# Edge scores of a graph layer: head sums of every fourth edge tile on ScalarE

## What is computed

```python
q = (x_norm @ Wq + bq).reshape(N, H, HD)      # N 1250, H 8, HD 64
k = (x_norm @ Wk + bk).reshape(N, H, HD)
scores = jnp.einsum('ehd,ehd->eh', q[origin], k[destination]) * SCALE
ws = scores * edge_weights
...
e = jnp.exp(ws - seg_max[origin])
```

## Time and profile before

| | |
|---|---|
| median of 3 runs | 2417.09 us |
| profiled execution, its own time | 2421.3 us |
| its span, first to last instruction | 2419.2 us |
| mean granted TensorE clock over the span | 0.846 of 2.4 GHz |
| stretch of `edge_scores` in it | about 527 to 802 us |
| busy over the span: PE / DVE / ACT / POOL | 79% / 52% / 20% / 33% |

### The profile page before, as it was taken

One profiled execution on the slowest core, in us unless ns is written; L12 is line 12 of the kernel. 1 busy time (PEld: TensorE's weight loads), 2 busy tenths in 40 slices (PEclk: granted clock), 3 DMA queues, 4 the chain that ended last, 5 costly groups with the idle time before them and its releaser, 6 DMA issues. The chain is left out here.

```text
span 2419.2 us, 23805 instructions
## 1 busy us (share of the span) xinstructions
PE 1921.7 (79%) x8175; PEld 1232.6 (51%) x8212; DVE 1265.2 (52%) x3309; ACT 476.3 (20%) x999; POOL 788.0 (33%) x697
## 2 busy tenths in 40 slices
PE   2499406976767579999896999989995999878876
PEld 2355203453333434444445888736554898655553
DVE  6565400438999679999102333433424274466423
ACT  3300000231111001111203222121212224343310
POOL 2077871026666067766202122101305301211100
PEclk8699757985676589999896899999997998887678
DMA  5022101026666156666101011011001000000001
GB/s 132 1 79 58 31 5 53 0 90 191 177 172 175 23 146 184 183 180 169 72 0 53 18 36 35 1 48 40 9 1 42 18 1 18 1 1 1 0 1 64
DMA packets 85241, 151.70 MB, mean 63 GB/s; under 512 B 34600, under 2 KB 39874, under 8 KB 85007
## 3 DMA queue, kind: packets, MB, share of 16 engines
q0 software_dynamic: 33280, 93.44, 14.5%
q1 hardware_dynamic: 51855, 56.91, 7.0%
HBM read 131.11 MB, written 19.02 MB: 62 GB/s over the span
## 5 line engine op out<-in xcount | busy, mean ns | idle before, releaser
L1074 POOL DMA_INDIRECT s_vbuf<-v_dram,s_recs x176 | 205.3, 1167 | 146.5 <-DVE s_vw L1102 75.3
L845 POOL DMA_INDIRECT s_kbuf<-k_dram,s_recs x176 | 167.5, 952 | 244.7 <-DMA s_recs<-rec_dram 149.3
L384 POOL DMA_INDIRECT rec_dram<-s_rec,s_rowid x160 | 199.7, 1248 | 143.0 <-issue 143.0
L1127 PE MATMUL s_pV<-s_vw,s_ohf 128*128 128x512 f32 x352 | 196.4, 640 | 0.0
L917 PE MATMUL s_psQ<-s_qh,s_ohT 128*128 128x512 f32 x176 | 111.8, 636 | 63.3 <-DVE s_prod L894 25.2
L894 DVE TENSOR_TENSOR s_prod<-s_psQ,s_kbuf 128x512 f32<-128x512 f32 x176 | 114.4, 683 | 24.5 <-remote 12.5
L1121 PE MATMUL s_pA<-s_ohd,s_ohb 128*128 128x512 bf16 (+1 forms) x491 | 117.0, 343 | 7.5 <-DVE s_ohf L1100 5.1
L1102 DVE TENSOR_TENSOR s_vw<-s_vbuf,s_W 128x512 f32<-128x512 f32 x176 | 120.5, 685 | 3.5 <-DMA s_vbuf<-v_dram,s_recs 3.5
L1121 PEld LDWEIGHTS s_pA<-s_ohd,s_ohb 128*128 128x128 bf16 x528 | 50.3, 98 | 127.0 <-issue 53.4
L618 PE MATMUL s_bank<-s_w,s_xnormT 128*128 128x512 f32 x240 | 114.9, 639 | 0.0
L684 PE MATMUL s_bank<-s_xnT,s_w 128*128 128x512 f32 (+1 forms) x96 | 37.2, 551 | 94.6 <-DMA s_w<-in_L_mix_WqkvT 94.6
(11 more groups left out here) (409 smaller groups left out, 4259.6 us busy)
## 6 DMA issues: line engine op xcount, KB each, us to landing
s_w<-in_L_ffn_W SPq DMA_DIRECT2D x16, 512.0 KB, 4.5
AT_dram<-s_A SPq DMA_DIRECT2D x10, 640.0 KB
s_w<-in_L_mix_WqkvT SPq DMA_DIRECT2D x3, 1024.0 KB
s_kbuf<-k_dram,s_recs POOLq DMA_INDIRECT x176
s_vbuf<-v_dram,s_recs POOLq DMA_INDIRECT x176
rec_dram<-s_rec,s_rowid POOLq DMA_INDIRECT x160
k_dram<-s_xn_rows SPq DMA_DIRECT2D x10, 256.0 KB
v_dram<-s_xn_rows SPq DMA_DIRECT2D x10, 256.0 KB
```

The lines of the kernel that those rows point to most:

```text
L384: nc.gpsimd.indirect_dma_start(out=b.rec_dram, out_offset=bass.IndirectOffsetOnAxis(ap=rowid[:, t:t + 1], axis=0), in_=rec[:, t, :], in_of ...
L845: nc.gpsimd.indirect_dma_start(out=kbuf[t % KB][:, :], out_offset=None, in_=b.k_dram, in_offset=bass.IndirectOffsetOnAxis(ap=recs[:, t, 2: ...
L1074: nc.gpsimd.indirect_dma_start(out=vbuf[t % VB][:, :], out_offset=None, in_=b.v_dram, in_offset=bass.IndirectOffsetOnAxis(ap=recs[:, t, 2: ...
L1127: nc.tensor.matmul(V[:, :], ohf[i][:, :], vw[i][:, :], start=False, stop=False, skip_group_check=True).then_inc(used[i], 1)
```

## The change

The tile with `t % 4 == 3`, the second of every odd pair, is multiplied into a buffer of its own (`act_prod`, two of them in turn), and VectorE does not reduce it. ScalarE sums it: eight copies of 64 columns onto themselves with an accumulated output that goes to `W[:, t, h:h+1]`. They come in two halves of four, behind the one-hot copies of the next two pairs: those of tile 4k+3 (pair 2k+1) behind the copies of pairs 2k+2 and 2k+3. The last tile's two halves stand behind the loop. The ring of `prod` shrinks from four buffers to three, and VectorE's waits are counted anew. TensorE's, GpSimd's and SyncE's instructions stay as they were.

```diff
-        sb, ps, s = b.tools(ctx, "loaded q_in qh ql identb oh0 oh1 tp0 tp1 ohT0 ohT1 qe0 qe1 prod0 prod1 red")
+        sb, ps, s = b.tools(ctx, "loaded q_in qh ql identb oh0 oh1 tp0 tp1 ohT0 ohT1 qe0 qe1 prod0 prod1 red act_red")
-        prod = [sb(f"prod{i}", [P, D]) for i in range(4)]
+        prod = [sb(f"prod{i}", [P, D]) for i in range(3)]
+        act_prod = [sb(f"act_prod{i}", [P, D]) for i in range(2)]
...
+            def head_sums(k, half):
+                t = 4 * k + 3
+                act.wait_ge(prod_s[1], t // 2 + 2)
+                for h in range(4 * half, 4 * half + 4):
+                    nc.scalar.activation(act_prod[k % 2][:, h * HD:(h + 1) * HD], act_prod[k % 2][:, h * HD:(h + 1) * HD], ACT.Copy,
+                                         accum_out=W[:, t, h:h + 1]).then_inc(s.act_red, 1)
...
                     nc.scalar.activation(ohT[i][:, :], psT[i][:, :], ACT.Copy).then_inc(ohT_s[i], 1)
+                if u >= 2:
+                    head_sums((u - 2) // 2, u % 2)
                 if u + 1 < NT:
                     high(u + 1)
+            for half in range(2):
+                head_sums(ST // 4 - 1, half)
+            act.wait_ge(s.act_red, H * (ST // 4))
...
-                    if t >= 4:
-                        dve.wait_ge(s.red, t - 3)
-                    nc.vector.tensor_tensor(prod[t % 4][:, :], psQ[i][:, :], kbuf[t % KB][:, :], ALU.mult).then_inc(prod_s[i], 1)
+                    if t % 4 == 3:
+                        out = act_prod[t // 4 % 2]
+                        if t >= 8:
+                            dve.wait_ge(s.act_red, H * (t // 4 - 1))
+                    else:
+                        out = prod[t % 4]
+                        if t >= 4:
+                            dve.wait_ge(s.red, 3 * (t // 4 - 1) + t % 4 + 1)
+                    nc.vector.tensor_tensor(out[:, :], psQ[i][:, :], kbuf[t % KB][:, :], ALU.mult).then_inc(prod_s[i], 1)
...
                     t = 2 * u + i
+                    if t % 4 == 3:
+                        continue
                     dve.wait_ge(prod_s[i], u + 2)
...
-            dve.wait_ge(s.red, ST)
+            dve.wait_ge(s.red, 3 * ST // 4)
```

## The result

The changed kernel takes 2422.94 us (median of 8 runs, 2421.49 to 2426.66), the kernel before beside it on the same chip 2415.82 us (8 runs, 2411.93 to 2419.83). The ratio is 1.0032 with a 95% interval of 1.0021 to 1.0043: slower by 0.3%, 7 us. The forecast was 2407 us with a range of 2396 to 2417, faster at 0.73. It is wrong in its number and in its sign. The profiled execution took 2422.19 us, its span 2420.4.

What follows compares the result with a forecast made beforehand. VectorE was taken to bound quiet pairs, with TensorE close behind at its lower clock. Terms -2.1 - 5.2 - 6.3 + 4.4 - 1.8 + 1.0 = -10.0 us gave 2407 us against the median of 2417.1, range 2396 to 2417.

Steps and rivals of the forecast that it cites:

- quiet pairs: From pair 10 on, pairs without late TensorE results: -5.2 us at the lower clock, -6.3 us at the higher.
- alternation: Products start 2.71 and 2.11 us apart in turn at the higher clock, 2.11 and 3.03 at the lower.
- granted clock: From pair 10 on, taken as 0.68: TensorE at its higher clock 36% of the time.
- first ten pairs: Start of the stage, with a low part of q: 3.31 us a pair becomes 3.01, together -2.1 us.
- tail: Last tile's eight sums on ScalarE end later than VectorE's last reduction did, delaying the next stage: +1.0 us.
- rival 3: ScalarE late: head sums of 0.55 us or more make it the bound, +13.4 us at 0.60, 2431 us; chance 0.07.
- stalls: Late TensorE results from pair 10 on: number kept at eleven, each about 0.4 us costlier, +4.4 us.
- rival 4: GpSimd's gathers take 1.35 us each, two 2.70: quiet pairs gain nothing, 2416 us; chance 0.06.
- rival 2: TensorE's clock stays high and VectorE alone bounds: -19.7 us, 2397 us; chance 0.20.

Runs made afterwards that it cites:

- e6: Changed kernel with only the first eight tiles gathered, all later products reusing their buffers: 2372.35 us, ratio 0.9796 to the kernel before.
- e2: Kernel before plus eight accumulating 64-column copies per two pairs on ScalarE, from a tile nobody else uses: 2421.91 us, ratio 1.0019.
- e3: Kernel before plus eight semaphore waits a pair on SyncE that nothing depends on: 2422.32 us, ratio 1.0021.
- e1: Changed kernel with ScalarE copying four columns per half instead of making four head sums: 2416.81 us, ratio 1.0002 to the kernel before.
- e5: Kernel before with only the first eight tiles gathered, all later products reusing their buffers: 2395.48 us, ratio 0.9884.
- e18: Changed kernel gathering only every second tile from the ninth tile on, fifth chip: 2373.30 us, ratio 0.9832 to the kernel before.
- e12: Changed kernel with gathers running four tiles ahead instead of eight, third chip: 2397.14 us, ratio 1.0001 to the kernel before.
- e16: Changed kernel with gathers running four tiles ahead instead of eight, fourth chip: 2420.39 us, ratio 1.0017 to the kernel before.
- e14: Changed kernel, nothing further edited, as a control on the fourth chip: 2424.58 us, ratio 1.0031 to the kernel before.

## Why the prediction was wrong

*What was right.* The quiet pairs: forecast 11.5 us of gain in 58 of them (5.2 and 6.3), measured 12.3 us in 62 by a slightly wider count. The alternation of 2.71 and 2.11 us at the higher clock came as written, at the lower one 2.97 and 2.11 to 2.18 for 3.03 and 2.11. The granted clock from pair 10 on was 0.70 (569 to 802 us), where 0.68 was taken. The first ten pairs took 36.6 instead of 37.8 us: 1.2 gained of 2.1. In the tail the last pair's product and the next stage's copy are 804.39 - 800.01 = 4.38 us apart instead of 3.62, 0.8 for the forecast's 1.0.

*ScalarE* (rival 3) was costed rightly. The view of the tile `act_prod` in the changed kernel:

```profile
L860 ACT ACTIVATE s_act_prod<-s_act_prod x352: 238/248/261, 537.0 to 803.0; 128x64 f32<-128x64 f32 x176
L860 ACT ACTIVATION_READ_ACCUMULATOR s_act_prod<-s_act_prod x352: 185/190/205, 537.2 to 803.2; 128x1 f32 x176
```

and the timeline of its end:

```profile
801.81 0.24 ACT L860 ACTIVATE s_act_prod<-s_act_prod 128x64 f32<-128x64 f32 x1
801.96 0.18 ACT L860 ACTIVATION_READ_ACCUMULATOR s_act_prod<-s_act_prod 128x1 f32 x1
802.05 0.24 ACT L860 ACTIVATE s_act_prod<-s_act_prod 128x64 f32<-128x64 f32 x1
...
803.15 0.18 ACT L860 ACTIVATION_READ_ACCUMULATOR s_act_prod<-s_act_prod 128x1 f32 x1
```

A sum follows the next after 0.24 us (taken 0.26), the accumulator's read is hidden, and the last ends at 803.33, 2.0 us behind the last product's end at 801.29 (forecast 2.2). With no stalls (e6) ScalarE carries all its sums and VectorE is busy for 179 of 180 us, so the sums are hidden in the quiet rounds, as I argued. That adding them still costs 0.2% beside the gathers (e2), as much as waits on an idle engine (e3), was not in the sum. The rule in the Trainium skill's "ScalarE: Activation LUTs", "Rules for kernel authors", wants additions on VectorE; no run here shows a price of the sums themselves that bears it out.

*The step that failed* is the stalls: "TensorE's instructions don't change, so I keep their number", and "Eleven stalls at about 0.4: +4.4 us". I had taken them for an outside disturbance at a fixed count, which only meets a thinner cover. They hang on GpSimd's gathers, and beside shorter quiet pairs they took more. The measured term is 39 - 19.6 = +19 us: a stall holds 3.0 instead of 1.8 us, so 11 of them cost 13 more instead of 4.4, and the two new ones cost 6. The head sums are not why a stall got longer: e1, without them, has 13 stalls and 17 x (4.72 - 2.52) = 37 us in them. Why a stall costs more beside a shorter round stays open. What could have told it stood in the earlier trace rows beside the earlier trace rows, and I had used them all: 77 periods in 229.6 us are one gather in 1.49 us, while quiet pairs issue one in 1.36 and GpSimd alone can do one in 1.25: the mean was below what both allow. I asked only whether GpSimd's own 2.50 us a pair would bound, and gave rival 4, in which the gathers have a pace of their own and the stage doesn't gain, 0.06. Its price in a quiet pair (2.70) is not what happened, since quiet pairs ran at 2.53; what was right of it is that the stage as a whole gains nothing. e1 has that result (1.0002), though not that rival's mechanism: its quiet pairs take 2.52.

*The sum by measured terms*: first ten pairs -1.2, pairs from 10 on 233.7 - 229.6 = +4.1, tail +0.8: +3.7 us between the two profiled executions' stages. The medians are 7.1 apart, these two executions' own times only 0.9; a stage of one kernel differs by some 4 from profile to profile, so the rest can't be placed.

*Without stalls* the mechanism pays: 23 us (e6 against e5), above even rival 2's 20. The changed kernel as it stands was not timed on the third chip, so what it does there is open.

## What to carry to other kernels

Before an engine that is saturated in quiet stretches is relieved, compare the mean rate of everything that runs at once with its rate in the quiet stretches. If the mean is slower, and what fills the difference comes at regular distances, then ask what else paces the stage before counting on the gain: here work taken off the visible bound came back as more and longer gaps. Take the suspect away in both kernels (here the gathers): if the change pays there and not in the full kernel, the gain is being given back, not missing. And an experiment on a chip where the reference itself runs otherwise shows nothing until the unchanged kernels stand beside it.

## What the runs showed of the hardware

- TensorE's results reach VectorE and ScalarE 1 to 5 us late, once in 5 to 7 pairs, while GpSimd issues indirect gathers of 128 rows at one per 1.25 to 1.36 us. With one issue per 2.44 us they never do (e18: 0 in 77 periods), nor with none (e5, e6), and in the stage `edge_sums` of the changed kernel, with mostly one gather per 1.5 us, the view of waits names none. Halving bytes or rows changes nothing (12 and 13 stalls).
- In a stall the semaphores of TensorE and of ScalarE's head sums are raised late, in steps of about 0.7 or 1.4 us (up to 5.5 us behind a head sum that has ended, in the changed kernel); of VectorE's 205 recorded events from pair 10 on none is over 0.02 us late. That TensorE's work is done by then is a reading, since its ends are modelled. Whether the recording has a part in it, is open.
- Four of the five chips of the experiments run the kernel before in 2416 to 2424 us, one in 2396, and there a kernel with all gathers has no late result (e12 there 0 stalls, the same kernel as e16 12 stalls; 2397.14 and 2420.39 us). Why, is open.
- 704 waits on SyncE that nothing depends on, of which at most the first of each eight has to wait, cost 0.21% [0.07, 0.36] (e3).
- The granted clock is lower where TensorE's rounds have gaps: 0.70 in the deep stretch with stalls (e14) and with waits for transfers instead (e12), 0.84 without either (e6, e18).
